# Where a conditioned causal attention kernel issues its big loads: slots behind a cell's block transfers, column-wise weights, and Wo on ScalarE's queue

## What is computed

```python
w = weights[conditions]
x = x + jnp.einsum('bct,bcd->bdt', x, w)
q, k, v = proj(x, Wq), proj(x, Wk), proj(x, Wv)
q = q * jnp.minimum(precision, 4.0)[:, None]
scores = jnp.einsum('bhqd,bhkd->bhqk', q, k) / np.sqrt(64)
attn = softmax(where(causal, scores, min))
out = jnp.einsum('bhqk,bhkd->bhqd', attn, v)
x = x + jnp.einsum('bsd,ed->bse', out, Wo)
```

## Time and profile before

| | kernel before |
|---|---|
| median of 3 runs | 1646.23 us |
| the profiled execution | 1646.84 us |
| its span | 1645.5 us |
| mean granted clock of TensorE | 0.984 |
| TensorE busy with matmuls | 1582.5 us (96%) |
| VectorE, ScalarE, GpSimd busy | 987.1, 817.6, 850.2 us |
| DMA | 341.46 MB, 208 GB/s on average |

### The profile page before, as it was taken

One profiled execution on the slowest core, in us unless ns is written; L12 is line 12 of the kernel. 1 busy time (PEld: TensorE's weight loads), 2 busy tenths in 40 slices (PEclk: granted clock), 3 DMA queues, 4 the chain that ended last, 5 costly groups with the idle time before them and its releaser, 6 DMA issues.

```text
span 1645.5 us, 23425 instructions
## 1 busy us (share of the span) xinstructions
PE 1582.5 (96%) x7563; PEld 1323.8 (80%) x7563; DVE 987.1 (60%) x1752; ACT 817.6 (50%) x2221; POOL 850.2 (52%) x748
## 2 busy tenths in 40 slices
PE   9999999999999999899998889999999989999999
PEld 7888888888887888788787777877887767888887
DVE  5835454443576677677675667666776645555553
ACT  6645555541565666466565456555666532222221
POOL 2454555452455555566564555555565434555552
PEclk9999999999999999999999999999999999999999
DMA  9867887757766656555778565565564687545442
GB/s 324 312 239 271 293 313 289 253 209 250 253 205 200 190 191 196 162 163 173 193 199 239 170 184 160 165 173 170 157 178 122 220 297 264 179 154 173 172 161 83
DMA packets 192811, 341.46 MB, mean 208 GB/s; under 512 B 23986, under 2 KB 112306, under 8 KB 186546
## 3 DMA queue, kind: packets, MB, share of 16 engines
q1 hardware_dynamic: 192690, 339.98, 63.7%
HBM read 184.70 MB, written 134.22 MB: 194 GB/s over the span
## 4 chain that ended last, share of the span: by engine, by line
PE 74%; DMA 8%; SPq 8%; issue 3%; ACT 3%; POOL 2%; DVE 2%; ACTq 0%; DVEq 0%; POOLq 0%
PE p_PJ L690 16%; PE p_PJ L691 16%; PE p_PJ L692 16%; PE p_SC L692 5%; PE p_SC L690 5%; PE p_SC L691 5%; DMA t_XL<-xtl_scratch 4%; SPq L1498 4%; PE p_PV L797 3%; ACT t_PP L1010 1%; PE p_PV L690 1%; POOL t_VV L1299 1%; PE p_PV L692 1%; PE p_PV L691 1%; PE p_LP L690 1%
## 5 line engine op out<-in xcount | busy, mean ns | idle before, releaser
L690 PE MATMUL p_PJ<-t_XH,t_WH 128*128 128x512 f32 x1008 | 402.2, 399 | 37.1 <-DMA t_XL<-xtl_scratch 34.4
L691 PE MATMUL p_PJ<-t_XL,t_WH 128*128 128x512 f32 x1008 | 400.6, 397 | 0.0
L692 PE MATMUL p_PJ<-t_XH,t_WL 128*128 128x512 f32 x1008 | 398.4, 395 | 0.0
L1010 ACT ACTIVATE t_PP<-t_PP,t_st 128x128 f32<-128x128 f32 x512 | 199.5, 391 | 186.2 <-DVE t_st L1183 184.7
L690 PEld LDWEIGHTS p_PJ<-t_XH,t_WH 128*128 128x128 f32 x1008 | 193.9, 192 | 76.6 <-issue 31.4
L1305 POOL TENSOR_TENSOR t_PP<-t_PP,t_st 128x512 f32<-128x512 f32 x128 | 133.2, 1041 | 218.4 <-DVE t_st L1187 218.4
L692 PEld LDWEIGHTS p_PJ<-t_XH,t_WL 128*128 128x128 f32 x1008 | 193.1, 192 | 42.0
L1199 DVE TENSOR_REDUCE t_AT<-p_PV 64x256 f32<-64x512 f32 x256 | 174.0, 680 | 78.9 <-ACT t_AC L1025 59.1
L691 PEld LDWEIGHTS p_PJ<-t_XL,t_WH 128*128 128x128 f32 x1008 | 194.1, 193 | 33.0
L1311 POOL TENSOR_TENSOR t_AT<-t_AT,t_AC 128x256 f32<-128x256 f32 x128 | 122.0, 953 | 129.4 <-DVE t_AT L1199 129.4
L1308 POOL TENSOR_TENSOR t_PS<-t_PT,t_PS 128x512 fp32r<-128x512 f32 x122 | 157.7, 1293 | 19.4 <-ACT t_PS L1017 19.4
(11 more groups left out here) (252 smaller groups left out, 3538.4 us busy)
## 6 DMA issues: line engine op xcount, KB each, us to landing
t_XH<-xth_scratch SPq DMA_DIRECT2D x56, 512.0 KB, 5.0
t_XL<-xtl_scratch SPq DMA_DIRECT2D x56, 512.0 KB, 5.7
t_PT<-t_TB SPq DMA_DIRECT2D x580, 32.0 KB, 1.9
v_scratch<-t_VR SPq DMA_DIRECT2D x64, 256.0 KB, 4.3
xth_scratch<-t_XH SPq DMA_DIRECT2D x16, 1024.0 KB, 4.0
xtl_scratch<-t_XL SPq DMA_DIRECT2D x16, 1024.0 KB, 6.4
t_VX<-v_scratch SPq DMA_DIRECT2D x32, 512.0 KB, 7.2
at_scratch<-t_AT SPq DMA_DIRECT2D x128, 128.0 KB, 4.3
```

What stands on the lines that cost most here:

```text
L690: pe.matmul(bank, lh, rh, start=first, stop=False, skip_group_check=goes_on)
L691: pe.matmul(bank, lh, rl, start=False, stop=False, skip_group_check=goes_on)
L692: return pe.matmul(bank, ll, rh, start=False, stop=last, skip_group_check=goes_on)
L1010: act.activation(PP[:, u, h, :], PP[:, u, h, :], ACT.Exp, bias=st[:, 0, u, h:h + 1], scale=1.0, accum_out=st[:, 1, u, h:h + 1]).then_inc(a ...
```

## The change

Nothing is computed differently.

- X loads: from eight single times to three, three and two in slots 9.5, 25.5 and 41.5 steps after the start of the group before (groups 1 and 9: four at 25.5 and four at 41.5).
- V loads move from 54 steps ahead of the group (36 ahead for group 1) to 6.5 ahead; for group 8 to 9.5 after its start. The splits move by 16 steps (32 for group 8).
- The later weights: W1 from 3 to 9.5 steps after the start of group 7; parts 1 and 0 of Wq at 25.5, of Wk at 41.5, part 2 of Wq at 57.5, of Wk at 73.5. Part 0 used to be loaded at 100 and 104. Each part now waits for the last block that reads its old columns.
- y loads from 4 to 9.5 steps after each cell's start in the last group, their splits with them.
- Wo's pieces: new times, both halves at once; pieces 4 to 7 are issued by ScalarE (`act_load_wo`), behind a wait for the last k block.
- The value product of the last item stands two steps later.
- GpSimd's first three sums of the first pair wait for the last block transfers (`l_P`) instead of the last AT stores; only the fourth, which writes the AT tile, still waits for the stores.

```diff
--- before.py
+++ after.py
@@ -389,29 +389,30 @@
                     last = n == 4 * NGRP - 1
                     half_at.put(a + (20 if last else 25.25) + 0.5 * k, P)
                     ptl_at.put(a + (20.75 if last else 26) + 1.5 * k, P)
-                    v = a + (25.25 + 3.25 * k if last else 29 + 4.5 * k)
+                    v = a + (27.25 + 3.25 * k if last else 29 + 4.5 * k)
                     own = v + (1.75 if n >= 4 * NGRP - 2 else (1.75, 8.5)[k])
                     for z in range(2):
                         pv_at.put(v, 2 * P + z)
                     other_at.put(v + 0.75, P)
                     own_at.put(own, P)
                     at_at.put(own + 1.25, P)
+
             if j and j != NG:
                 for i in range(8):
-                    X_load.put(t0 - STEPS + (12 + 5 * i if j == 1 else 24 + 4 * i if j == NG + 1 else (1, 6, 17, 22, 33, 38, 49, 54)[i]), (j, i))
+                    X_load.put(t0 - STEPS + ((25.5, 41.5)[i // 4] if j in (1, NG + 1) else (9.5, 25.5, 41.5)[i // 3]), (j, i))
             for k in range(2):
-                V_load.put(t0 + (-11, 2.75)[k] if j == 0 else t0 - STEPS + (28 if j == 1 else 10), (j, k))
+                V_load.put(t0 + ((-11, 2.75)[k] if j == 0 else 9.5 if j == NG else -6.5), (j, k))
             for u in range(GB):
-                v_split.put(t0 + (17, 19, 27.75, 28.75)[u] if j == 0 else t0 - STEPS + 51.75 + u + 14 * (u // 2), (j, u))
+                v_split.put(t0 + ((17, 19, 27.75, 28.75)[u] if j == 0 else (19.75 if j == NG else 3.75) + u + 14 * (u // 2)), (j, u))
         t = T_ATT + STEPS * (NG - 1)
-        for d, item in ((57, (2, 1)), (57.25, (2, 2)), (64.5, (3, 1)), (70, (3, 2)), (100, (2, 0)), (104, (3, 0))):
+        for d, item in ((25.5, (2, 1)), (25.5, (2, 0)), (41.5, (3, 1)), (41.5, (3, 0)), (57.5, (2, 2)), (73.5, (3, 2))):
             W_load.put(t + d, item)
         W1_load = At()
-        W1_load.put(t + 3, 0)
+        W1_load.put(t + 9.5, 0)
 
 
         for b in range(GB):
-            t = T_END - STEPS + 4 + 16 * b
+            t = T_END - STEPS + 9.5 + 16 * b
             y_load.put(t, b)
             y_high.put(t + 10, b)
             y_low.put(t + 11.5, b)
@@ -436,10 +437,10 @@
                 O_split.put(O_cell(8 * c + k), (c, k))
                 if k >= 4:
                     O_add.put(O_cell(8 * c + k) - 6, (c, k))
-        for k, t in ((1, T_END - 22), (3, T_END - 34), (0, T_END - 7), (2, T_END + 2),
-                     (6, T_END + 11), (5, T_END + 19), (4, T_END + 31), (7, T_END + 43)):
+        for k, t in ((3, T_END - 38.5), (1, T_END - 22.5), (0, T_END - 6.5), (2, T_END + 9.5),
+                     (6, T_END + 27), (5, T_END + 31), (4, T_END + 38), (7, T_END + 43)):
             O_fetch.put(t, (k, 0))
-            O_fetch.put(t + 3, (k, 1))
+            O_fetch.put(t, (k, 1))
 
 
         yp_load, xp_load, S_add, A_high, A_low, R_at, f_at, c_at, x_at, o_store = (At() for _ in range(10))
@@ -656,6 +657,9 @@
             tiles, half = {0: ((WH[0], WL[0]), 0), 1: ((VH[0], VL[0]), 0), 2: ((WH[0], WL[0]), 1), 3: ((WEH, WEL), 0),
                            4: ((WH[1], WL[1]), 0), 5: ((XH[0], XL[0]), 0), 6: ((WH[1], WL[1]), 1), 7: ((XH[0], XL[0]), 1)}[k]
             return tuple(t[:, 4 * half:4 * half + 4, :] for t in tiles)
+
+        def wo_half(k, low):
+            return wo_tile(k)[low].bitcast(f32).rearrange("p d e -> p (d e)")
 
 
         def qk_piece(m):
@@ -938,6 +942,11 @@
             if n >= 4:
                 act.wait_ge(s_V[n % 4], 16 * (n // 4))
             act.activation(v_slot(n), bank[:], ACT.Copy).then_inc(act_v, 1)
+
+        def act_load_wo(k, low):
+
+            act.wait_ge(pe_k, 64)
+            act.dma_start(wo_half(k, low), (woh_d, wol_d)[low][k]).then_inc(l_O[k], 16)
 
         def act_program():
             for tick in range(T_START * TICK, (T_OUT + 4) * TICK):
@@ -1009,6 +1018,9 @@
                     for h in range(2):
                         act.activation(PP[:, u, h, :], PP[:, u, h, :], ACT.Exp, bias=st[:, 0, u, h:h + 1],
                                        scale=1.0, accum_out=st[:, 1, u, h:h + 1]).then_inc(act_e, 1)
+                for k, low in O_fetch(tick):
+                    if k >= 4:
+                        act_load_wo(k, low)
                 for P in half_at(tick):
                     n = P // 2
                     act.wait_ge(l_P, 160 * (n + 1))
@@ -1323,8 +1335,7 @@
                             pool.wait_ge(dve_A, 7 * q)
                         else:
                             pool.wait_ge(s_O, 32 * 32)
-                            for k in range(2):
-                                pool.wait_ge(s_at[k], 16 * 64)
+                            pool.wait_ge(l_P, 160 * 64)
                         pool.tensor_tensor(sums(0), a21, a22, ALU.add).then_inc(pool_S, 1)
                     elif i == 1:
                         pool.wait_ge(pool_S, 4 * q + 1)
@@ -1333,6 +1344,9 @@
                         pool.wait_ge(pool_S, 4 * q + 2)
                         pool.tensor_tensor(a21, a11, a21, ALU.subtract).then_inc(pool_S, 1)
                     else:
+                        if q == 0:
+                            for k in range(2):
+                                pool.wait_ge(s_at[k], 16 * 64)
                         pool.tensor_tensor(sums(3), a12, sums(1), ALU.subtract).then_inc(pool_S, 1)
                 for q, i in x_at(tick):
                     b, half = ((1, 0), (0, 1), (1, 1))[i]
@@ -1423,10 +1437,9 @@
                 if n < 2 and part == 0:
 
                     sp.wait_ge(pe_P, 7 * (NP - 3) + 2 * n + low + 1)
-                elif n == 2 and part == 1 and low == 0:
-                    sp.wait_ge(pe_q, 4 * NG)
-                elif n == 3 and part == 1 and low == 0:
-                    sp.wait_ge(pe_k, 4 * NG)
+                if n >= 2 and low == 0:
+
+                    sp.wait_ge((pe_q, pe_k)[n - 2], 4 * NG - (3, 2, 0)[part])
                 to = (WH, WL)[low][n % 2][:, :, cols].bitcast(f32)
                 sp.dma_start(to, qk_half(n, low, cols)).then_inc(l_W[n][part], 16)
 
@@ -1525,6 +1538,7 @@
             sp.dma_start(wol_d[k][:, cols], OL[:].bitcast(f32)).then_inc(s_O, 16)
 
         def sp_load_wo(k, low):
+
             if k == 3 and not low:
                 sp.wait_ge(s_O, 32 * 32)
                 sp.wait_ge(pool_vl, GB * NGRP)
@@ -1532,9 +1546,7 @@
                 sp.wait_ge(pe_pv, 16 * (NGRP - 1))
             elif k in (0, 2):
                 sp.wait_ge(pe_q, 64)
-            elif k != 3:
-                sp.wait_ge(pe_k, 64)
-            sp.dma_start(wo_tile(k)[low].bitcast(f32).rearrange("p d e -> p (d e)"), (woh_d, wol_d)[low][k]).then_inc(l_O[k], 16)
+            sp.dma_start(wo_half(k, low), (woh_d, wol_d)[low][k]).then_inc(l_O[k], 16)
 
         def sp_load_pair(q):
             g, b = divmod(batches(q)[0], GB)
@@ -1627,7 +1639,8 @@
                 for c, k in O_split(tick - TICK):
                     sp_store_wo(c, k)
                 for k, low in O_fetch(tick):
-                    sp_load_wo(k, low)
+                    if k < 4:
+                        sp_load_wo(k, low)
                 for q, i in o_store(tick):
                     b, half = {1: (0, 0), 3: (1, 1), 4: (1, 0), 5: (0, 1)}[i]
                     sp.wait_ge(dve_c, 6 * q + i + 1)
```

## The result

The changed kernel takes 1588.45 us (median of 4 runs, 1585.5 to 1589.09) against 1646.3 us (4 runs): a ratio of 0.9645, 95% interval 0.9628 to 0.9661. The profiled execution took 1588.61 us with a span of 1587.3, 58.2 us less than the one of before. The mean granted clock is 0.995 (0.984 before). The forecast was 1576.5 in a range of 1567 to 1598: the time lies in the range, but 12 us above the forecast and outside its own range.

A forecast was written before the change was run, and what follows sets the result against it. TensorE, busy 96%, was taken to lose time in waits, mainly for late X loads, and half clock after them. Gains 52.6 + 1.7 + 4.0 + 4.6 + 7.5 = 70.4 off 1646.84 gave 1576.4, predicted as 1576.5 us, range 1567 to 1598.

The forecast's parts named there:

- own range: Narrower range around the forecast of 1576.5 us: 1567 to 1583; the forecast had chance 0.70, nine tenths of it within this.
- X loads: Group starts: last load issued 13.33 us earlier, all 13 TensorE waits go with their half clock; gain 52.6 us.
- the cross-check: Second count of the X gain: 61.9 us lost over 14 groups, less 7.5 in groups 7 to 9, gives 54.4.
- Three loads in a slot cost nothing: X slots: three loads instead of two ahead of block transfers; bounds 0 to 1.4 us per slot, 0 taken.
- The cover of 3.9 us behind the turn: Per cell: block transfers have 12.1 us to land before VectorE's next turn, normally need 8.2; 3.9 us to spare.
- The rival of 1597: Half of the 40 X slots push the next block transfers past their cover by about 1 us: + 20 us; chance 0.11.
- V, cell 0, cell 60: V move costs 0; cell 0's 1.6 us wait goes, gain 1.7 us; y's load first in cell 60, gain 4.6.
- Groups 7 to 9: Later weights' slots: 7.5 us lost before, 3.5 still lost (between 0 and 7.5), gain 4.0.
- lateness 1.6, 3.2, 4.8 against 3.9: Groups 7 to 9: SyncE's issues exceed a cell by 1.6 us, three cells on end, against 3.9 us of cover.
- The end: Last cells and Wo: of 11.1 us lost 3.6 are left, gain 7.5 us, between 0 and 9.
- The rule that spoke against the change: At the end: issuing from several engines saves only sequencers' time, all share 16 DMA engines; the tail keeps its 11.1 us.
- this rival: The tail keeps its waits: Wo's four megabytes slow the output stores SyncE waits for; 1584 us, chance 0.12.

The follow-up runs named there:

- e1: The kernel before with the new X load slots and nothing else: 1599.87 us, ratio 0.9714 to the kernel before.
- e10: The changed kernel with six of a group's eight X loads in slot 25.5 and two in 41.5, in 12 groups: 1593.71 us.
- e2: The changed kernel with columns 0 to 255 of the later Wq and Wk as one load for high and one for low: 1583.86 us.
- e5: e2 with W1 in two slots, its half of Wq at 9.5 and its half of Wk at 25.5: 1581.97 us, run again 1582.66.
- e6: The changed kernel without loading Wo's pieces 4 to 7, computing with what stands in the tiles: 1576.7 us.
- e3: The changed kernel with Wo's pieces 4 to 7 issued by SyncE at the same nominal times: 1587.69 us.
- e4: The changed kernel with Wo's pieces 6 and 5 issued later, at T_END + 33.5 and 37 instead of 27 and 31: 1589.29 us.
- e7: The changed kernel with Wo's pieces 6, 5, 4, 7 spread to T_END + 27, 37, 43 and 52: 1587.74 us.
- e9: e5 with the two megabytes of each of Wo's pieces 4 to 7 issued 5.5 steps apart: 1579.69 us.
- e8: The changed kernel with all eight X loads of a group in slot 25.5, in 12 groups: 1623.32 us.

## Why the prediction came out as it did

- **X loads, right.** Forecast 52.6 by the waits and 54.4 by the cells. Measured: the 14 groups lose 53.0 us less with groups 7 to 9 losing 8.8 instead of 7.5, so 54.3 come from the X loads, and 1.3 more from the half clock behind the wait that ended at 1256.70, which the cross-check left out. That is 55.7; the cross-check, which counts from starts alone, was the better number. e1 shows that one line does it.
- **Three loads in a slot cost nothing, right** for 1.6 MB, for the 2.1 MB of group 1, and in e1 for 2.6 MB (three X, two V). The cover of 3.9 us behind the turn is confirmed by e10. The rival of 1597 (half of the slots late by 1 us) doesn't occur: there is no wait from 397 to 790.
- **V, cell 0, cell 60, right**: the waits of 1.6 and 2.9 us are gone, and none took their place.
- **Groups 7 to 9, wrong.** Forecast 3.5 us left; 8.8 are lost. The step that failed is "lateness 1.6, 3.2, 4.8 against 3.9". Its left side was short: I summed the issues of the loads, but SyncE stays held back into the block transfers (8.3 us for 6.2), so that cells 27 and 28 started 2.3 and 6.2 us late and cell 27's AT store went out 4.3 us late. Its right side was the wrong limit: 3.9 us is the cover of the turn, while the reader that comes out last is the AT reduce behind it, through the AT store that SyncE issues behind the transfers. By an estimate from these rows, that store, undelayed, would be issued at 786.8 and land at 791.4, with VectorE there at 792.7: 1.3 us of cover, 1.9 with what TensorE has in front. 4.3 - 1.3 = 3.0, and VectorE waited 3.08. The 6.2 of cell 28 did not show at its turn because this wait had pushed the turn back too (791.42 to 809.00, 17.6 us for 13.3). e2 and e5, which carry the same bytes in fewer issues or spread over more slots, take 4.6 and 6.5 us off at the median; their output products start 4.3 and 6.2 us earlier.
- **The end, wrong.** Forecast 3.6 us left of 11.1; by the count above 14.6 are lost, where it gives 11.7 before. The first half of the argument held: output 0's store lands in 2.7 us (7.58 before), the transfers of cell 63 start at their turns, and the `t_PS` wait of 6.0 is gone. The wait for the first x1 load, which I left at 1.7, is 2.5. What failed is the clause that the last stores matter less since only the fourth sum waits for them, with "in its gaps" for ScalarE's issues. I priced the issues of the Wo loads (0.5 us each), but not what their 4 MB do to the AT store issued beside them (8.5 us, 3.0 without them in e6) nor to those after it (11.8, 14.1 and 13.9, against 5.2, 8.6 and 4.5 in e6). The bytes had moved from in front of the output store to in front of the AT stores. e3, e4 and e7 move them again, and the waits move with them while the time stays; e6 takes them away, and 10 us of the 14.6 go.
- **The rule that spoke against the change fits.** The Trainium skill, "DMA: Bandwidth & Descriptors", section "Issuing engines are not separate DMA queues", says that issuing from another engine saves sequencer time only. e3 puts the loads back on SyncE and comes out within 1 us, in another order of issue. I had given this rival 0.12 and 1584. With groups 7 to 9 also keeping all they lost, the prediction's own terms give 1576.5 + 7.5 + 4.0 = 1588.0, where 1588.45 was measured, but that nearness is luck: both stretches lost more than before, by 1.3 and 2.9 us, and the X loads brought 3.1 more than their term. The miss of 12 us is itself a balance: groups 7 to 9 and the end cost 5.3 and 10.4 us more than forecast, the X loads and the opening brought 3.1 and 0.45 more. Both missed terms are of one kind: small transfers that someone waits for, behind bulk loads.

The difference between 8.8 by cells and 5.4 by waits in groups 7 to 9 is half clock behind the waits of 2.5 and 3.0 us (some 1.5 us each, as in the earlier trace rows; the granted clock is 0.95 from 780 to 850) and the modelled ends. What the changed `l_P` wait of GpSimd's sums and the later value product of the last item bring by themselves wasn't tried.

## What to carry to other kernels

When bulk loads are moved to where no one waits for them, list every small DMA that is issued within the next few microseconds per megabyte, with its reader, and size the cover of the tightest one: the limit is often not the transfer in sight but a store behind it that frees a tile. A load that has slack is worth splitting into single megabytes apart from each other (the likely gain of e9); another engine's queue brought nothing here. Fewer, wider loads (here 256 columns instead of two of 128) are worth trying before moving anything.

## What the runs showed of the hardware

- A load of all rows at 128 columns (512 bytes each) holds its issuer once two are ahead of it: 0.59, 0.66, 2.82, 2.17 us for the four of W1, and the first block transfer behind them took 1.68 us where 0.51 to 0.6 is usual. Eight X loads of 512 KB in a row took only 0.43 to 0.75 us each (e8; one of 1.62 among the six of e10): what holds SyncE isn't bytes alone.
- A small DMA on SyncE's queue waits behind megabytes on ScalarE's: 128 KB took 8.5 us with 2 MB issued ahead of it and 2 MB right behind, 8.9 with 2 MB in all and 3.0 with none (e7, e6). The Trainium skill, "DMA: Bandwidth & Descriptors", section "Queues, rings and completion order", says that each DMA engine takes turns between its queues packet by packet. The trace agrees: 144 packets of ScalarE's queue to 140 of SyncE's from 1286 to 1289. That protects a small store little here, because its packets hold 1 KB and Wo's 8 KB, and in that time SyncE's queue moved 0.14 MB and ScalarE's 1.05. The later stores stand behind loads of their own queue as well.
- Over 10 us the DMA engines moved 395 and 411 GB/s at a share of 1.04 with Wo's pieces, the AT stores and the outputs mixed; 299 with the narrow weight loads at 794 to 800, at a share of 1.08.
